# Column norm of a LoRA-adapted embedding table: from squaring the summed table to three separate sums

## The reference, cut to what matters

```python
base = weight[x]                              # weight: 32000 x 512, x: 32 x 128
after_A = lora_A.T[x]                         # lora_A: 16 x 32000
result = base + after_A @ lora_B.T * 2.0      # lora_B: 512 x 16
direction = weight + lora_A.T @ lora_B.T * 2.0
direction_norm = sqrt(sum(direction * direction, axis=0))   # one number for each of 512 columns
h = result * magnitude * direction_norm
```

## Time and profile before

| What | Value |
|---|---|
| median of the runs | 1555.16 us |
| the profiled execution's own time | 1555.47 us |
| its span on the core | 1553.7 us |
| PE busy | 1400.4 us |
| DVE busy | 1189.6 us |
| ACT busy | 909.8 us |
| POOL busy | 456.1 us |
| end of `embed`'s last copy (L365, 253.09 + 0.69) | 253.8 us |
| first instruction of `attend` (L588) | 255.8 us |

### The profile page before, as it was taken

How to read it: one execution, slowest core, us unless ns; L and a number is a source line. 1 busy time by engine, 2 the same in 40 slices (tenths; PEclk the granted TensorE clock), 3 DMA queues, 4 the chain that set the end, 5 groups by cost and what they waited for, 6 DMA issues and landing times.

```text
span 1553.7 us, 36325 instructions
## 1 busy us (share of the span) xinstructions
PE 1400.4 (90%) x13322; PEld 1179.3 (76%) x13386; DVE 1189.6 (77%) x2350; ACT 909.8 (59%) x1692; POOL 456.1 (29%) x526
## 2 busy tenths in 40 slices
PE   4576775999999999599999999999999999999997
PEld 2232433777777777399999999889899898999996
DVE  5598895889888888568656778778777787777776
ACT  3788784777777777433323656666565666533331
POOL 4445446444454421102211121111111110044333
PEclk9999999999999999699999999999999999999999
DMA  8999995223222211221112587777777877444365
GB/s 304 341 330 296 327 315 114 57 64 81 62 71 71 67 49 43 84 100 52 40 42 78 192 280 238 255 260 241 259 247 265 280 241 244 167 145 145 135 221 184
DMA packets 76011, 271.44 MB, mean 175 GB/s; under 512 B 10320, under 2 KB 10832, under 8 KB 71680
## 3 DMA queue, kind: packets, MB, share of 16 engines
q1 hardware_dynamic: 59472, 226.03, 42.2%
q0 software_dynamic: 16432, 44.05, 11.1%
HBM read 226.27 MB, written 43.78 MB: 174 GB/s over the span
## 4 chain that ended last, share of the span: by engine, by line
PE 28%; DVE 11%; issue 6%; ACT 6%; DMA 5%; SPq 0%; ACTq 0%; POOL 0%; DVEq 0%; POOLq 0%
PE up_ps L1662 6%; PE up_ps L1664 5%; PE up_ps L1663 5%; PE down_ps L1663 3%; PE down_ps L1664 3%; PE down_ps L1662 3%; DVE w_split L1437 3%; ACT w_split L1352 3%; DMA slot_rows<-y_rows 3%; DVE xT_lo L1428 2%; DMA w_stage<-packed 2%; DVE h L1573 1%; PE up_ps L1696 1%; DVE w_split L1434 1%; PE up_ps L1691 1%
## 5 line engine op out<-in xcount | busy, mean ns | idle before, releaser
L1662 PE MATMUL up_ps<-xT_hi,w_split 128*128 128x256 f32 x1280 | 366.4, 286 | 16.2 <-DVE xT_lo L1428 8.2
L1664 PE MATMUL up_ps<-xT_hi,w_split 128*128 128x256 f32 x1280 | 362.7, 283 | 0.0
L1663 PE MATMUL up_ps<-xT_lo,w_split 128*128 128x256 f32 x1280 | 362.6, 283 | 0.0
L1662 PEld LDWEIGHTS up_ps<-xT_hi,w_split 128*128 128x128 f32 x1280 | 245.5, 192 | 19.3 <-DVE xT_lo L1428 8.3
L1663 PEld LDWEIGHTS up_ps<-xT_lo,w_split 128*128 128x128 f32 x1280 | 245.6, 192 | 1.3
L1664 PEld LDWEIGHTS up_ps<-xT_hi,w_split 128*128 128x128 f32 x1280 | 245.5, 192 | 0.0
L1374 ACT ACTIVATE h_hi<-h 128x256 fp32r<-128x256 f32 (+1 forms) x192 | 80.2, 418 | 264.9 <-DVE h L1573 204.9
L1325 POOL DMA_INDIRECT xr<-x_rows,slot_tokens x71 | 71.5, 1007 | 425.9 <-PE xT_ps L1757 381.4
L393 PE MATMUL norm_ps<-a_split,b_split 96*128 96x500 f32 x256 | 140.1, 685 | 56.1 <-DVE W L294 32.0
L294 DVE TENSOR_TENSOR W<-W,norm_ps 128x1000 f32<-128x1000 f32 x128 | 146.8, 1187 | 39.6 <-PE norm_ps L393 33.0
L1352 ACT ACTIVATE w_split<-w_stage 128x1408 fp32r<-128x1408 f32 (+1 forms) x123 | 169.1, 1411 | 3.8 <-PE down_ps L1664 1.8
(11 more groups left out here) (280 smaller groups left out, 3077.6 us busy)
## 6 DMA issues: line engine op xcount, KB each, us to landing
W<-table_c SPq DMA_DIRECT2D x32, 2000.0 KB, 15.3
w_stage<-packed SPq DMA_DIRECT2D x80, 704.0 KB, 5.6
w_stage<-packed SPq DMA_DIRECT2D x40, 768.0 KB, 5.2
xr<-x_turned SPq DMA_DIRECT2D x32, 512.0 KB, 3.8
slot_rows<-y_rows SPq DMA_DIRECT2D x32, 512.0 KB, 6.2
x_rows<-x SPq DMA_DIRECT2D x32, 256.0 KB, 2.0
x_turned<-x2T SPq DMA_DIRECT2D x32, 256.0 KB, 3.9
out<-H SPq DMA_DIRECT2D x32, 256.0 KB, 3.9
```

Source lines behind the costliest of these rows:

```text
L1662: pe.matmul(out, a_hi, b_hi, start=first, stop=False)
L1663: pe.matmul(out, a_hi, b_lo, start=False, stop=False)
L1664: return pe.matmul(out, a_lo, b_hi, start=False, stop=last)
```

## The change

The square of a sum is expanded: the sum over the vocabulary of (W + 2AB)^2 is the sum of W^2, plus 4 times the sum over rank r of B[r] (A W)[r], plus 4 times B' (A A') B. So the table itself is squared and summed, A W is one accumulated product of 16 x 512, and A A' one of 16 x 16.

- The table is read as it lies in HBM, `table`, row by row: a chunk is now 640 vocabulary rows, five in each partition (10,240 bytes), 1.31 MB. There are 50 chunks and six slots; six chunks are a trip; eight trips and two loose chunks, which are loaded in tiles of 128 x 512. `table_c` is gone. A comes once, in two pieces, as `a_all`.
- PE multiplies each of the five tiles of a chunk (128 vocabulary rows) by A's 16 columns into one of four 32-partition strips of `cross_ps`, in plain float32, and in trips 1 to 3 also A by itself into `gram_ps`.
- ACT squares the chunk in place after PE has read it, without summing; DVE adds the squares into `acc`, 2560 numbers in a partition. The last four chunks go by tiles of 512.
- At the end PE sums the partitions of `acc`, of the product of `cross_ps` and B, and of the Gram term in `total_ps`.
- The splitting of A and B is gone from ACT, POOL and DVE. POOL issues its 32 gathers of A one behind the other; ACT takes the last four sequences' results.

The diff, cut to its core:

```diff
-CHUNK = 1000
+CHUNK_TILES = 5
+CHUNK = CHUNK_TILES * P
 CHUNKS = VOCAB // CHUNK
-HALF = CHUNK // 2
+SLOTS = 6
+TRIPS = CHUNKS // SLOTS
...
+        BY_TILE = CHUNKS - 4
+        LOOSE = SLOTS * TRIPS
...
         def _(sp):
...
             def load_w(c, q):
-                sp.wait_ge(squared, (c + 1) * KT)
-                sp.dma_start(W[:, q, :, :].rearrange("p k n -> p (k n)"), table_c[bass.ds(c, 1), :, :].rearrange("c p n -> (c p) n")).then_inc(w_in[q], 16)
+                if not isinstance(c, int) or c >= SLOTS:
+                    sp.wait_ge(summed, c - SLOTS + 1)
+                sp.dma_start(W[:, q, :, :].rearrange("p j d -> p (j d)"),
+                             table[bass.ds(c * CHUNK, CHUNK), :].rearrange("(p j) d -> p (j d)", p=P)).then_inc(w_in[q], 16)
...
         def _(pool):
...
+            pool.wait_ge(w_in[SLOTS - 1], 16 * TRIPS)
+            for i in range(EARLY_ROWS - 2):
+                early_row(i)
+            pool.wait_ge(terms_made, TOTAL)
             pool.tensor_tensor(root[:, :], total[:, :], half[:, :], ALU.pow).then_inc(rooted, 1)
...
         def _(act):
...
+            def squares(c, q):
+                act.wait_ge(crossed, c + 1)
+                act.activation(W[:, q, :, :], W[:, q, :, :], ACT.Square).then_inc(squared, 1)
...
         def _(dve):
...
-            def add_products(c, g, q, k):
-                if k == 0:
-                    dve.wait_ge(w_in[q], (g + 1) * 16)
-                dve.wait_ge(normed, 2 * KT + c * KT + k + 1)
-                w = W[:, q, k, :].rearrange("p (h n) -> p h n", h=2)
-                dve.tensor_tensor(w, w, norm_ps[k % 2][:, :, 0:HALF], ALU.add).then_inc(added, 1)
...
+            def add_squares(c, q):
+                dve.wait_ge(squared, c + 1)
+                after(dve, summed, c)
+                dve.tensor_tensor(acc[:, :, :], acc[:, :, :], W[:, q, :, :], ALU.add).then_inc(summed, 1)
...
+            def add_tile(c, j):
+
+                dve.wait_ge(squared, done(c, j))
+                dve.wait_ge(summed, added(c, j) - 2)
+                half_no = (c * CHUNK_TILES + j) % 2
+                dve.tensor_tensor(acc[:, half_no, :], acc[:, half_no, :], W[:, c % SLOTS, j, :], ALU.add).then_inc(summed, 1)
...
         def _(pe):
...
+            def strip(n):
+                return slice(DH * (n % GROUPS), DH * (n % GROUPS) + RANK)
+
+            def cross(n, q, j, last=False):
+
+                return pe.matmul(cross_ps[strip(q + j), :], a_all[:, n, :], W[:, q, j, :], start=False, stop=last,
+                                 skip_group_check=True)
+
+            def gram_tiles(tiles, last):
+                for n in tiles:
+                    mm = pe.matmul(gram_ps[strip(n), 0:RANK], a_all[:, n, :], a_all[:, n, :], start=False, stop=last, skip_group_check=True)
+                return mm
```

More of the change, by code:

```diff
@@ L67, in add_table_row, with embed @@
                             compute_op=ALU.add).then_inc(h_in[i % EARLY_ROWS], 16)
-def embed(nc, ids, table, table_c, lora_a, lora_a_t, lora_b_t, magnitude_t, attn_ws, H, rows_i, h_in, wT, w_scale, S_bc, ident, ones):
+def embed(nc, ids, table, lora_a_rows, lora_a_t, lora_b_t, magnitude_t, attn_ws, H, rows_i, h_in, wT, w_scale, S_bc, ident, ones):
     with ExitStack() as ctx:
@@ L88, in embed @@
         a_group_t = sb("a_group_t", [P, P])
+        a_all = sb("a_all", [P, CHUNKS * CHUNK_TILES, RANK])
         b_rep = sb("b_rep", [P, D])
[L90 to L98, removed]
+        zeros = sb("zeros", [DH, D])
+        W = sb("W", [P, SLOTS, CHUNK_TILES, D])
+        acc = sb("acc", [P, CHUNK_TILES, D])
+        product = sb("product", [P, D])
+        gram = sb("gram", [P, RANK])
+        gram_b = sb("gram_b", [RANK, D])
+        diag = sb("diag", [P, KT, P])
         total = sb("total", [P, KT])
@@ L260, in _ @@
+            act.wait_ge(const_ready, 4)
             for g in range(4):
                 trip(g)
-            with act.Fori(0, trips - 5) as g:
+            with act.Fori(0, TRIPS - 5) as g:
                 trip(g + 4)
-            trip(trips - 1)
+            trip(TRIPS - 1)
+            for c in range(LOOSE, CHUNKS):
+                for j in range(CHUNK_TILES):
+                    squares_of_tile(c, j)
+            act.wait_ge(lora_done, TRIPS)
+            for j in range(SEQ_GROUP):
+                act.activation(H[:, SEQS - SEQ_GROUP + j, :], lora_ps[j][:, :], ACT.Copy).then_inc(lora_free, 1)
@@ new lines, in _ @@
+            with dve.Fori(0, TRIPS - 6) as g:
+                trip(g + 5)
+            trip(TRIPS - 1)
+            for c in range(LOOSE, CHUNKS):
+                for j in range(CHUNK_TILES):
+                    add_tile(c, j)
+            dve.scalar_tensor_tensor(out=product[:, :], in0=cross_ps[:, :], scalar=2.0 * LORA_SCALE, in1=b_rep[:, :],
+                                     op0=ALU.mult, op1=ALU.mult).then_inc(terms_made, 1)
+            dve.wait_ge(b_in, 16 * (GROUPS + 1))
+            dve.wait_ge(totalled, 1)
@@ L386, in products @@
[L386 to L397 removed]
+            pe.wait_ge(const_ready, 4)
@@ new lines, in add_up @@
+            def add_up(source, rows, first, last):
+                for k in range(KT):
+                    mm = pe.matmul(total_ps[:, 8 + k:9 + k], source[:, k * P:(k + 1) * P], ones[0:rows, 0:1], start=first and k == 0, stop=last,
+                                   skip_group_check=True)
+                return mm
+            pe.wait_ge(a_in[0], 16)
+            trip(0)
+            pe.wait_ge(a_in[1], 16)
+            for g in range(1, 4):
+                trip(g)
+            trip(4)
+            pe.wait_ge(terms_made, GRAM)
@@ L425, in _ @@
+            last = CHUNKS * CHUNK_TILES - 1
+            pe.wait_ge(summed, added(CHUNKS - 1) - 1)
+            add_up(acc[:, (last - 1) % 2, :], P, False, False)
+            pe.wait_ge(summed, added(CHUNKS - 1))
+            add_up(acc[:, last % 2, :], P, False, False)
+            pe.wait_ge(terms_made, PRODUCT)
+            add_up(product, P, False, True).then_inc(totalled, 1)
             for k in range(KT):
```

312 lines of the change are left out of this document (150 added, 162 removed).

## The result

The changed kernel takes 1529.84 us (median of four runs, 1528.98 to 1530.31) against 1555.28 us for the kernel before, run beside it: a ratio of 0.983, 95% interval 0.982 to 0.984. The profiled execution took 1529.94 us, its span 1527.6. `attend` starts at 227.6 us in place of 255.8.

What follows compares the result with a forecast made beforehand. Embed was taken as bound by 74.8 MB of transfers and a DVE-PE loop of nearly equal length. Last addition at 219 plus 10.6 puts attend at 229.6 against 255.8, so 1555.5 - 26.2 gives 1529 us; 8-in-10 range 1515 to 1547.

Steps and rivals of the forecast that it cites:

- Transfers: In embed, 71.9 MB in place of 74.8 at 350 GB/s (ends 286 and 362); last tile landed at 212 us.
- DVE's addition: In embed's chunk loop, DVE's addition of 2560 columns takes 2.85 us, at the least 2.7.
- The two meet ... I take 219: End of embed's loop: DVE alone ends at 217 us, transfers give 215.5; each sometimes waits, so last addition at 219.
- rival D: In embed, transfers are faster than 362 GB/s and DVE alone sets the end: 1517 to 1523 us; chance 0.08.
- The end chain: After DVE's last addition: PE's sums 4 us, a copy 0.3, root's start to the end of S_bc 4.3.
- Then 2.0 to `attend`: Between the end of S_bc and attend's start: 2.0 us, as in the earlier trace.
- What follows `attend`'s first instruction isn't touched: After embed nothing changes, so the gain is only attend's earlier start: 229.6 against 255.8 us, 26 us.
- A: Rival, embed: PE sets the pace at its lower clock, 1551 to 1569 us, taken as 1552; chance 0.10.
- B: Rival, embed: strips don't run beside each other at 512 columns, ten passes in a row, 1579 us; chance 0.04.
- C: Rival, embed: the row-wise table read doesn't hold its rate; at 286 GB/s 1571 us; chance 0.04.
- E: Rival, embed: transfers were already the bound, so only the debt at the end, 12 us, is gained: 1543; chance 0.06.
- The rule of the Trainium skill on weight loads: PE in embed: loads overlap running matmuls only with differing row groups; otherwise each chunk pays ten loads in the open.

Runs made afterwards that it cites:

- experiment 7: Kernel before, A loaded into a_f only for the first four chunks, 56 of 64 small loads gone: 1544.01 us, ratio 0.992.
- experiment 1: Changed kernel with the 28 copies of lora_ps into H done by ACT in place of DVE: 1518.71 us, ratio 0.977 to the kernel before.
- experiment 4: Changed kernel with ACT making the four attention weights ternary later in its own order: 1523.63 us, ratio 0.978 to the kernel before.
- experiment 5: Changed kernel with all eight POOL gathers of table rows issued ahead of the root, not six: 1522.18 us, ratio 0.978 to the kernel before.
- experiment 6: Changed kernel with all table-by-A products put into the first strip of cross_ps instead of four: 1569.13 us, ratio 1.008 to the kernel before.
- experiment 3: Changed kernel with attention weights loaded one by one behind the seventh to tenth chunk, used one trip later: 1526.20 us, ratio 0.981 to the kernel before.

## Why the prediction came out right, and where it didn't

The median is 0.8 us from the forecast, but by terms that cancel: that it is so near is luck. The sum put `attend` at 229.6, and it was 227.6; the terms:

- **Transfers: wrong, though the mean agrees.** I took 350 GB/s, between ends of 286 and 362. At a full share they run at 394 to 412 in 20 to 60 us and at 399 in 160 to 180. From 60 to 200 us the mean is 355, close to my 350, but because the slots came back late (a share of 0.88 to 0.97 from 80 to 160 us), not because that is the engines' speed. PE started on the last tile at 206.9 us; the forecast had it landing at 212. The upper end was a rate that the small loads of A had held down (experiment 7): I named them as a reason, and then capped the rate by a row that contained them. Of the two figures of the Trainium skill that I had cited (DMA: Bandwidth & Descriptors, Bandwidth), the runs go past the 358 GB/s and up to 423, near its 425.
- **DVE's addition: right.** 2.820 us, forecast 2.85. The tokens' copies 0.681 (0.68), the tile's 0.681. The rounding took 1.28 in place of 2.154 us, and scaling the group 0.22 in place of 0.7. The means that I had taken were mixtures, as the kernel before shows in order of time at two of its four roundings:

```profile
87.57 2.32 POOL L186 TENSOR_TENSOR a_split<-a_f,a_split 32x1000 fp32r<-32x1000 f32 x1 [3.45 <-ACT a_split L224]
88.36 2.61 DVE L324 TENSOR_SCALAR H<-H,w_inv 128x2048 f32<-128x2048 f32 x1
...
116.12 2.31 POOL L186 TENSOR_TENSOR a_split<-a_f,a_split 32x1000 fp32r<-32x1000 f32 x1 [3.85 <-ACT a_split L224]
116.14 3.38 DVE L324 TENSOR_SCALAR H<-H,w_inv 128x2048 f32<-128x2048 f32 x1
```

Both roundings end 1.1 us after POOL's subtraction L186 has ended; the other two, which started as it ended or later, took 1.35 and 1.28. So they stood until POOL was done, and the change removed L186. POOL's gathers don't do this: beside them the group's scaling took 0.22 (55.11 us, kernel after).
- **"The two meet ... I take 219": this step failed.** DVE's last addition ended at 212.15, 6.9 us earlier. 2 of them are what I added for the meeting with the transfers, and nothing of it came. The other 4.9 lie in the sum for DVE alone, 217 "at the earliest": it started on the seventh chunk at 52.4 us in place of 54, and needed 159.8 in place of 163. That DVE alone sets the end is the mechanism of rival D, to which I had given 0.08. Experiments 1 and 4 show it: what DVE is spared of waits moves the end (5.8 of 6.5 us), and of work the half. D's time, 1517 to 1523, didn't come only because of the next three terms, 7.5 us in all with what lies outside the span. Even the 159.8 us are near the forecast by luck: DVE worked for 150.5 of them and stood still for 9.3, of which 6.5 at the roundings (experiment 4). These waits, which I had nowhere, stand against roundings and groups that were cheaper by 6.9 us and instructions that overlap a little.
- **The end chain: nearly right.** From the last addition to the end of `S_bc` 9.4 us, forecast 8.6. PE's sums ran at the lower clock (granted 0.50 from 212 to 222 us).
- **Then 2.0 to `attend`: failed, 6.1.** I took the distance of the earlier trace rows as a constant of the change of blocks. It is the last gather that holds it up (experiment 5). I had said that the two gathers behind the root "end before `S_bc`"; even their issue ended 0.5 us behind it, at 222.0, and their landing later still.
- **What follows `attend`'s first instruction isn't touched: true of the code, not of the time.** It took 1297.9 us before and 1300.0 after, and 1296.6 to 1300.8 in the ten experiments with the same code in it. So 2 us of any such sum are not to be had from one execution, and an effect of a few us is read at the start of `attend`, not in the time.

In the sum: 6.9 less, then 0.8, 4.1, 2.1, and 0.5 outside the span, makes 0.6 more than 1529.3. The rivals: A fell, since ten passes take 1.89 us at the full clock, which is granted in most of the stage once the chunks come evenly (1.00 from 140 to 180 us), and 3.40 in the fourth chunk, at 25.85 us, after a stretch granted 0.50 (22 to 26 us); both are covered. Its premise, that PE was at the lower level for all of the old `embed`, stands on durations alone (the column said 1.00). They bear it out: the tokens' product took 1.24 us for eight passes there and 1.15 for sixteen in the kernel after, where 1.00 is granted (154.68 us). A granted 1.00 can stand over slow passes early in an execution: the first chunk after took 3.57 us under it (from 7.77 us), against the 1.89 of later ones. B's condition didn't come, and when made by hand gave 1569 (I had 1579). C fell: the row-wise read holds its rate, though it is no faster than the old one without the loads of A (384 and 382 GB/s in experiment 7). E fell: transfers and loop were both bounds before; without A's loads the first goes, and the second leaves 1544. One slip of the text itself: the upper end is 1539 under the bounds and 1541 where the chances are given; nothing here depends on it.

The rule of the Trainium skill on weight loads that I had weighed (TensorE: Matmul & The Clock Gate, Part 3: Packing small matmuls) stays contradicted at 512 columns as I had read it. PEld of the kernel after:

```profile
162.72 0.13 PEld L387 LDWEIGHTS cross_ps<-W,a_all 128*16 128x16 f32 x8 [2.20 <-DMA W<-table]
```

Eight loads are over in 0.13 us, while the first matmuls run, and all ten passes take 1.89 us, little more than four times the 0.43 us of one pass (experiment 6): the loads add nothing that can be seen. The same section also lets a load into the background weight buffer overlap, which I had left out; whether that is what happens here the trace doesn't tell.

## What to carry to other kernels

Where two bounds lie close, sum each engine alone from the last wait that is sure, and take the larger; add nothing for their meeting without a row that shows it. A rate read from a stretch holds the overhead of everything else in the queue, so it is no upper end once that is taken out. A mean over few instructions can hide two durations: look at each one, and at what ran beside it. Before a distance is carried over as a constant (a change of blocks), look up what ended last on every engine and queue ahead of it.

## What the runs showed of the hardware that I had not expected

- Four float32 products into four strips of 32 columns run beside each other at 512 columns too: 1.89 us for ten passes against 4.3 in one strip.
- Loads of 62.5 KB into sixteen partitions lower the rate of the queue that they are in: 339 GB/s of its own time with them, 382 without (60 to 200 us, experiment 7; one profiled execution each).
- POOL's gathers of 64-byte rows can cost much more in one execution than in another: 16.8 and 2.0% of the DMA engines' time for 0.19 and 0.16 MB (20 to 60 us), and from 60 to 80 us 14.7% with 328 GB/s (experiment 1), 8.1% with 370 (kernel after) and 1.8% with 411 (experiment 3), each at a full share. Why is open.
- A block ends 5.4 to 6.6 us after the issue of its last indirect DMA, if nothing else is later.
- A tensor_scalar of 128x2048 on DVE that started while POOL ran a subtraction (L186) stood until that had ended: 2.61 and 3.38 us in place of 1.28. So did the small addition L300, whose operands are both in SBUF: 1.46 us (226.52) in place of 0.15, until L186 ended at 227.96. The additions L294, which take one operand from PSUM, kept their time beside it (1.20 us at 212.67).
